# One gathered tile in seven leaves TensorE, and a fourth last tile is fetched row by row

## The reference

```
e   = edge_attr @ We + be                 # edge_attr is one number per edge
m   = relu(x[src] + e)                    # 40000 x 512
agg = segment_sum(m, dst)
h   = ((1 + eps) * x + agg) @ W1 + b1
h   = relu(batch_norm(h) * gamma + beta)  # over all nodes
x   = relu(h @ W2 + b2)
```

## Time and profile before

| | |
|---|---|
| median of 3 runs | 1813.56 us (1788.38 to 1814.72) |
| profiled execution, its own time | 1810.87 us |
| span of that execution | 1809.0 us, mean granted TensorE clock 0.903 |
| TensorE (PE) busy | 1442.0 us, 80% |
| VectorE (DVE) busy | 1305.0 us, 72% |
| GpSimd (POOL) busy | 969.9 us, 54% |
| ScalarE (ACT) busy | 275.3 us, 15% |
| DMA | 301.49 MB, mean 167 GB/s; 51.4% of 16 engines in the gather queue |

### The profile page before, as it was taken

The page is one execution under the profiler, slowest core; times in us unless marked ns, Lnnn a source line. Parts: engine busy times, 40 slices in busy tenths (PEclk is TensorE's granted clock), DMA queues, the critical chain, the costliest instruction groups (busy, mean ns, idle before and its releaser), DMA issues.

```text
span 1809.0 us, 23422 instructions
## 1 busy us (share of the span) xinstructions
PE 1442.0 (80%) x7672; PEld 831.3 (46%) x7672; DVE 1305.0 (72%) x2351; ACT 275.3 (15%) x652; POOL 969.9 (54%) x1026
## 2 busy tenths in 40 slices
PE   1468888987947988897884788988795588988888
PEld 0235555554523545454541445555453245545544
DVE  5977788776547777786664777778754677877777
ACT  1301101011600100010240010110151001101014
POOL 4365566663165666666145666666606556666630
PEclk9979999997967999998895999999897789998989
DMA  6465566654465566666355666666626556666643
GB/s 224 146 175 165 158 174 174 170 168 128 127 193 165 168 178 172 178 176 180 101 186 151 182 175 175 181 170 184 181 87 210 156 168 175 173 184 172 176 142 117
DMA packets 102621, 301.49 MB, mean 167 GB/s; under 512 B 20595, under 2 KB 21747, under 8 KB 102493
## 3 DMA queue, kind: packets, MB, share of 16 engines
q0 software_dynamic: 81280, 266.40, 51.4%
q1 hardware_dynamic: 21212, 33.52, 5.6%
HBM read 287.05 MB, written 12.80 MB: 166 GB/s over the span
## 4 chain that ended last, share of the span: by engine, by line
PE 62%; DVE 20%; issue 11%; another core or an unknown queue 6%; ACT 0%; DMA 0%; DVEq 0%
PE y_ps L1711 21%; PE pair_ps L1664 16%; DVE rows L1278 13%; PE h_ps L1813 7%; PE y_ps L1860 7%; PE uT_ps L1766 2%; DVE src_onehot L1096 2%; PE uT_ps L1773 1%; PE uT_ps L1759 1%; PE uT_ps L1748 1%; PE y_ps L1735 1%; DVE onehot L1086 1%; DVE rows L1125 1%; DVE u L1285 1%
## 5 line engine op out<-in xcount | busy, mean ns | idle before, releaser
L695 POOL DMA_INDIRECT rows<-node_table,src_fast x960 | 910.1, 948 | 601.8 <-issue 256.4
L1278 DVE SCALAR_TENSOR_TENSOR rows<-We_ps,negw_fast,rows 128x512 f32<-128x512 f32 x1016 | 694.2, 746 | 0.4
L1664 PE MATMUL pair_ps<-rows,onehot 128*32 128x512 f32 x2504 | 418.5, 674 | 173.3 <-DVE rows L1278 98.5
L1711 PE MATMUL y_ps<-table_parts,src_onehot 128*128 128x512 f32 x1792 | 526.0, 431 | 31.1 <-issue 29.9
L1711 PEld LDWEIGHTS y_ps<-table_parts,src_onehot 128*128 128x128 f32 x1792 | 336.8, 200 | 343.6 <-issue 270.5
L1278 DVE SCALAR_TENSOR_TENSOR rows<-We_bc,negw_fast,y_ps 128x512 f32<-128x512 f32 x224 | 167.0, 746 | 314.7 <-remote 201.7
L1664 PEld LDWEIGHTS pair_ps<-rows,onehot 128*32 128x32 f32 x2504 | 61.8, 112 | 310.5 <-issue 210.4
L1813 PE MATMUL h_ps<-uT,W_sb 128*128 128x128 f32 x1152 | 152.6, 291 | 36.8 <-issue 36.2
L1813 PEld LDWEIGHTS h_ps<-uT,W_sb 128*128 128x128 f32 x1152 | 145.0, 204 | 52.6 <-issue 51.2
L1096 DVE TENSOR_TENSOR src_onehot<-y_ps,src_bc 128x512 fp32r<-128x512 f32 x224 | 153.1, 685 | 0.0
L847 ACT COPY pair_sb<-pair_ps 128x512 f32<-128x512 f32 x76 | 44.4, 584 | 632.6 <-PE pair_ps L1664 301.4
(11 more groups left out here) (201 smaller groups left out, 859.1 us busy)
## 6 DMA issues: line engine op xcount, KB each, us to landing
be_bc<-node_table SPq DMA_DIRECT2D x1024, 2.0 KB
rows<-node_table,src_fast POOLq DMA_INDIRECT x960
b_bc<-node_table SPq DMA_DIRECT2D x512, 2.0 KB
node_table<-rows SPq DMA_DIRECT2D x29, 256.0 KB, 2.4
x_now<-x_pad SPq DMA_DIRECT2D x10, 512.0 KB, 7.1
W_sb<-W SPq DMA_DIRECT2D x4, 1024.0 KB
rows<-W SPq DMA_DIRECT2D x16, 256.0 KB
out<-rows SPq DMA_DIRECT2D x8, 256.0 KB
```

Of the source, the lines that this page charges most:

```text
L695: nc.gpsimd.indirect_dma_start(rows[:, slot, :], None, source, bass.IndirectOffsetOnAxis(places[:, t:t + 1], 0)).then_inc(landed[q], 16)
L1278: last = nc.vector.scalar_tensor_tensor(rows[:, slot, :], We_of, negw_fast[:, t:t + 1], row, ALU.mult, ALU.max)
L1664: last = nc.tensor.matmul(pair_ps[h][WIN * win:WIN * (win + 1), :], onehot[:, h, tile - h * PAIR, :], rows[:, slot, :], start=t in firsts, ...
L1711: last = nc.tensor.matmul(y_ps[k % 2][:, :], src_onehot[:, first + at, :], table_parts[:, part, at, :], start=(part, at) == PLACES[0], sto ...
```

## The change

Quads 0 to 5 of steps 1 to 8 keep their TensorE tile; that of quad 6 (tile 24 of the step) is gathered by GpSimd like the others. Step 8 joins the steps whose tile 31 comes row by row. It is the fourth such tile of a layer and goes to `b2_bc`.

```diff
-    BY_ROW = [2, 4, 6]
+    BY_ROW = [2, 4, 6, 8]
...
     def pe_quads(l, i):
-        return tuple(range(USED_RUNS)) if i in SORTED else ()
+        return tuple(range(USED_RUNS - 1)) if i in SORTED else ()
```

## The result

The changed kernel takes 1837.8 us (median of 4 runs, 1835.4 to 1840.1 but for one disturbed run of 2454.7) beside 1808.2 us for the kernel before (median of 4): a ratio of 1.0188 with the 95% interval [1.0129, 1.0246], so 1.9% slower where 1796 us, 1% faster, was forecast. The profiled execution took 1835.58 us against 1810.87, 24.7 us more.

The account below looks back on a forecast made before the run. TensorE was taken as the bound, with room on GpSimd, though further gathers lengthened steps. Terms -54 - 5 + 42 - 1 = -18 us on 1810.87 gave 1793, set to 1796 us by the runs' median; range 1750 to 1857.

Parts of the forecast that it names:

- Products that go: TensorE's L1711: eight products fewer for each of 32 tiles, 1.70 us a tile, -54 us (bounds 0 to -95).
- One-hot matrices: VectorE's L1096: 32 matrices fewer, 0.16 us each on the chain, -5 us (bounds 0 to -22).
- Gathers: GpSimd: 28 more gathers at 1.49 us each, slope read from the windows, +42 us (bounds 0 to +70).
- the same work in all of them: Windows between L1285: TensorE and VectorE have equal work in all steps, so differing lengths were read as the gathers' price.
- Row by row: SyncE's fourth row fetch, 128 more DMAs a layer: ends with 28 us to spare, 0 (contention 5 us at most).
- Setup: Two of 18 copies of spread source numbers go, at 0.6 us: -1 us (none to 1.5).
- Messages: VectorE's 32 messages stay, reading a gathered slot in place of PSUM; both forms take 746 ns: 0.
- The sum: All terms on the whole kernel: -54 - 5 + 42 - 1 = -18 us, forecast 1796 us, 1.0% faster.
- The gathers set the pace, and TensorE's relief gives nothing: Rival: GpSimd's stream of gathers sets a step, fewer products don't shorten it; 1855 us, 2.3% slower; chance 0.20.
- GpSimd's room takes the gathers: Rival: GpSimd's 66.8 us a layer of slot waits absorb the gathers, +42 falls away; 1754 us, 3.3% faster; chance 0.25.
- The clock: Rival: less busy TensorE falls to its lower clock, +44 us, 1840 us; sign a mean granted clock below 0.88; chance 0.05.
- The late row: Rival: the fourth row tile comes 10 us late for VectorE in each layer, +40, 1836 us; chance 0.05.

Follow-up runs that it names:

- e4: Changed kernel with tile 24 of steps 1 to 8 not fetched at all: 0.9851 and 0.9863 of the kernel before, 0.9928 on the quick chip.
- e3: e2 with GpSimd also gathering tile 24 of steps 1 to 8, VectorE still using TensorE's products: 1.0220 of the kernel before.
- e2: Kernel before with the fourth row tile added, seven tiles still on TensorE: 1.0023 and 0.9991 of the kernel before.
- e1: Changed kernel without the fourth row tile, so step 8's last tile is still gathered by GpSimd: 1.0141 of the kernel before.
- e10: Changed kernel with a memset on GpSimd, waited for, after each quad of gathers: 1.0096 of the kernel before, 1.1231 on the quick chip.
- e6: Changed kernel with gathers of 1 KB rows, half the bytes, from step 1 on: 1.0119 of the kernel before, 1.0135 on the quick chip.
- e11: Changed kernel with gathers of 64 rows in place of 128 from step 1 on: 1.0148 of the kernel before, 0.9892 on the quick chip.

## Why the prediction was wrong, point by point

- **The step that failed is "Products that go", -54 us.** Relief alone measured -31 and -23 us, next to the gathers -14 us with zero in its interval, and some -6 us on the quick chip. The share of L1711 in the chain was taken as time that goes with the products. But VectorE waits for a signal, and the earlier trace rows already showed a message 5 us behind the shown end of its products: such a wait doesn't end with the eight products. TensorE did become 58.5 us less busy, but its idle time with no shown reason grew by 99 us, and by 65 in e4, where nothing is gathered in exchange. A share of the chain has no term for that. The measured relief lies between the lower bound, 0, and the middle.
- **One-hot matrices, -5 us**: contained in the relief just given; not measured apart.
- **Gathers, +42 us**: 35 us for 32 gathers with all of TensorE's work (e3 less e2), 1.1 us each where 1.49 was taken, so 31 us for the change's 28; with TensorE relieved 52 us for 36 (e1 less e4), so 40 us for 28. Both are within the bounds. Right by luck in part: the slope was read from windows of which the longest carried nothing to the end (e2). And the windows of the earlier trace rows that begin with step 0 are not like the others:

```profile
554.04:595.39 41.35, 29.02 (x163) 16.32 (x162) 27.77 (x46) 3.93 (x9) 25.59 (x27) 0.88 0.59 169
```

As step 0 has no TensorE tile in quad 6, they hold 26 gathers and not 25, and some 163 of TensorE's products where the others have about 184. Without these three the mean is 38.2 us, and the price from 24 to 25 gathers 2.0 us in place of 2.50. The prediction's "the same work in all of them" doesn't hold for them.

- **Row by row, 0**: right, 1.0023 and 0.9991, in time by 34 us. **Setup, -1**: the copies of the shown form fell from 10 to 8, too small for a run to show. **Messages, 0**: 744 and 743 ns, right.
- **The sum**: in the group that takes it apart, relief beside gathers -14, gathers +35, row tile +4 (zero in its interval), so +25 us where -18 was forecast. These are differences along one chain of kernels that ends at e1, and e1 stands at +24, so that they add up is no check. The first measurement of the change itself was +30 us.
- **The rivals.** "The gathers set the pace, and TensorE's relief gives nothing" comes nearest, at the point that the prediction gave for it, though the time lies 17 us below its 1855: it decides when relief is worth less than 1.3 us a tile, and it is worth 1.0 alone and 0.4 beside the gathers. Its signs are there: windows with 25 gathers longer, GpSimd waiting as before. Its mechanism, GpSimd's stream of gathers setting the pace, is right on the quick chip, but is not shown on the kind of chip of the forecast: there 170 us more on GpSimd left the total as it was (e10). "GpSimd's room takes the gathers": the room is real, the gathers cost all the same. The clock gave its sign, 0.865, and its 1840 us is the number nearest to the measured one. But e4 was faster than before at 0.885, and e3, which takes nothing from TensorE, slower at 0.883 (the kernel before: 0.903 and 0.899). A product of L1711 took 440 ns in the mean where it took 431: over 1536 of them that is 14 us of busy time, an estimate of what the clock cost there. So less work alone didn't set the clock, and the clock alone not the time; no run held the clock, so its share stays open. The late row: refuted.
- **Still open**: by what a gather costs its 1.1 to 1.4 us on the 1790 us kind. Halving the bytes and the packets left most of it (e6, e11), and it isn't the message's source (e3 reads y_ps as before). GpSimd's own time isn't settled: in the total the pauses cost nothing, in the steps 49 us (e10). Open too is what makes TensorE sit idle with no shown reason and its signals come late there, and neither on the quick chip.

## What to carry to other kernels

An engine's share of the chain is its time only if the waits on it end with its shown work, and if nothing else takes the place of the work that goes. Where a waiting engine starts microseconds after the shown end of what it waits for, cost a relief of that engine at no more than half until a run with the work simply left out has been seen. A price per piece read from windows of different load has to be checked at the window's far end: what one window gains, the stretch behind may take. And costs of two engines that hand buffers to each other are measured one without the other, and then together.

## What the runs showed of the hardware

- One program takes 1478 to 1480 us in some groups and 1788 to 1808 us in others, with the instructions of the computing engines about as long (in the changed kernel a message 742 and 743 ns, a gather 947 and 948, a product 430 and 440) and the bound on another engine. Three things differ. TensorE's signals for a gathered tile come 0.01 us after the shown end on the quick chip, 1.9 to 2.6 us in the median on the other (1.2 to 1.6 us in the kernel before). TensorE's idle time with no shown reason is 0 in all eight traces of the quick chip and 196 to 297 us in the twelve others. And SyncE, which only issues DMAs in this kernel, issues its row fetches more slowly: the same 128 DMAs, in the changed kernel on the quick chip and on the other, at the start of layer 1:

```profile
405.09 51.37 SPq L607 DMA_DIRECT2D be_bc<-node_table  x128
```
```profile
501.78 98.00 SPq L607 DMA_DIRECT2D be_bc<-node_table  x128
```

All the 16 fetches of that kernel take 51 to 52 us each on the quick chip, 70 to 98 on the other, and in e10 there 61 to 84. So it isn't TensorE alone that is slower there between its instructions. The mean granted clock differs too, 0.948 and 0.865 for the same kernel.

- A change can cost about the same share on both (1.0149 and 1.0188) with another engine at the bound: the same pauses on GpSimd gave 1.1231 and 1.0096.
- The Trainium skill (Perfetto Trace Analysis, DMA Instruction — SWDGE (GPSIMD)) says that the shown end of such an instruction is the end of writing its descriptors, not of moving data. The trace agrees: with half the bytes (e6) a gather is shown with 945 ns, with all of them 947.
